# Local attention of the last stage: one matmul per head in quarter and eighth tiles, in place of head pairs padded with zeros

## The chip, the cores and the metric

The kernel runs on one core of a Trainium2 chip. The core has a matrix engine (TensorE; PE in the profile, its weight loads PEld), a vector engine (VectorE, DVE), an activation engine (ScalarE, ACT), a general engine (GpSimd, POOL) and a queue that issues DMAs (SyncE, SP). Each takes its own instructions strictly in the order in which they were written, and they wait for one another on semaphores. The metric is the time of one execution on the device in microseconds.

## The reference, cut to what matters

The network has eight parts on activations of 16 sequences of 256 tokens by 128 features. The change is in the last one, a small transformer with 6 layers, 16 heads of 64 and a window of 32 tokens, applied to each sequence:

```python
def local_attention(q, k, v):                 # (b, 16 heads, 256, 64)
    ...                                       # 8 windows of 32 queries; each sees 64 keys: the window before and its own
    sim = jnp.einsum('bhwie,bhwje->bhwij', bq, bk2) * QK_SCALE
    sim = jnp.where(mask, -jnp.finfo(sim.dtype).max, sim)
    attn = jax.nn.softmax(sim, -1)
    out = jnp.einsum('bhwij,bhwje->bhwie', attn, bv2)
...
    q = l2norm(q) * qs
    k = l2norm(k) * ksc
    q = q * cos * scale + rotate_half(q) * sin * scale      # rotate_half: (x1, x2) -> (-x2, x1)
    k = k * cos * inv + rotate_half(k) * sin * inv
    out = local_attention(q, k, v)
    return out.transpose(0, 2, 1, 3).reshape(b, n, INNER) @ Wo
```

Each layer adds this to the activations, then a feed-forward part (layer norm, 128 to 2 x 341, gelu gate, back to 128).

## The kernel before, in words

The last stage is the method `L3f`. A unit `u` is one sequence in one layer, 6 x 16 = 96 units in a row. A unit has two tiles `t` of 128 tokens. All is float32; the activations stand transposed in `Z`.

Each engine has a function (`pe`, `act`, `dve`, `pool`) that writes out its instructions for two units at a time. The lists at the end of these functions are an order written by hand: the work of unit 2i+1, 2i+2, 2i+3 and 2i+4 is interleaved in it, and nothing reorders it. One unit passes through these steps:

- `project` (L2559): 12 matmuls of 128x512 for q, k and v, into three PSUM banks in turn. ACT squares the q and k parts (L2768), DVE sums the squares per head (L2954), ACT takes the inverse root (L2776, L2778), DVE scales into `raw` (L2971, `norm`). ACT copies the v part (L2787), and SP puts it into windows (`vw`) by DMA.
- Rotation on POOL, four halves of a unit (q and k of each tile): `sine` (L3155) multiplies the swapped halves of each head by the sine table into `t2`, `cosine` (L3164) multiplies `raw` in place, `add` (L3172) adds. The swap is made by two instructions, each of 16 heads x 32.
- `turn_qk` (L2572): eight groups of four 128x128 transposes through one PSUM bank; after each group ACT copies the bank to SBUF (`turned`), q to `qz` (L2799) and k to `kT` (L2803), and the next group waits for the copy.
- `scores` (L2588): `qz` holds for each pair of heads and each window a block whose two diagonal quarters are the q of the two heads and whose other two are zero. So one matmul with 128 rows of contraction and 64 columns of weights does both heads of a window: 32 matmuls for each tile, in two column halves of the array.
- DVE adds the mask (L2982), takes the maximum (L2988) and subtracts it (L2996); ACT takes the exponential (L2810), DVE the sum (L3002), the reciprocal (L3008) and the product (L3014) in `sm`.
- `turn_p` (L2601): 8 transposes of 128x128 into PSUM banks 4 and 5; ACT spreads them to `pT` (L2820) with zeros in the same pattern, by four copies of 64 partitions each (`spread`).
- `values` (L2614): again 32 matmuls of 128 rows by 64 columns. ACT copies the outcome to `oT` (L2830), `project_out` (L2627) multiplies by Wo, then come the layer norm's matmuls (L2634, L2640) and, once in two units, the feed-forward part (L2653, L2660, L2669).

`halves` is ((partitions 0 to 63, 0), (partitions 64 to 127, 1)). A float32 matmul shows as two weight loads and two matmul records on TensorE, a transpose as one of each.

## Time and profile before

| what | us |
|---|---|
| the three runs | 4803.81, 4824.44, 4836.79 (median 4824.44) |
| span of the profiled execution | 4799.2 |
| the last stage within it | from about 1556 to the end |
| busy in the span: PE, DVE, ACT, POOL | 4554.0, 3761.7, 3501.1, 3692.6 |

A span is the time from the first to the last instruction of the profiled execution. A busy time of PE counts matmuls from the reading of their operands to their modelled end, so a PE that is busy all the time need not be streaming all the time.

### The profile page before, as it was taken

How to read it: one execution, taken by the hardware profiler on the slowest of the kernel's cores; microseconds unless marked ns; L12 is line 12 of the kernel's file. 1: busy time of each engine (PE TensorE's matmuls, PEld its weight loads, DVE VectorE, ACT ScalarE, POOL GpSimd, SP SyncE). 2: the span in 40 equal slices, each digit the busy share in tenths (PEclk: the TensorE clock that was granted, in tenths of full speed). 3: DMA queues.
4: the chain of work that ended last, by engine and by line, in shares of the span. 5: the costliest groups of instructions: out<-in, count | busy, mean ns of one | idle time of the engine just before them, and what ended most of it. 6: DMA issues, size and time to landing. Idle time of an engine off the chain costs nothing.

```text
span 4799.2 us, 114895 instructions
## 1 busy us (share of the span) xinstructions
PE 4554.0 (95%) x44512; PEld 3128.6 (65%) x44512; DVE 3761.7 (78%) x5226; ACT 3501.1 (73%) x6738; POOL 3692.6 (77%) x2336
## 2 busy tenths in 40 slices
PE   7998999987887799999999999999999999999997
PEld 5666768874443466666666666666666666666665
DVE  6776556658999688888888888888888888888885
ACT  3454756557775688888888888888888888888885
POOL 2222334438998999999999999999999999999993
PEclk9898999998999999999999999999999999999998
DMA  2000000004332222232222322232322322322222
GB/s 79 1 2 1 2 1 1 1 1 168 150 142 106 55 63 63 56 85 70 54 67 65 75 68 55 68 75 61 68 64 67 76 53 66 80 64 63 62 56 52
DMA packets 164292, 289.06 MB, mean 60 GB/s; under 512 B 44063, under 2 KB 61351, under 8 KB 159655
## 3 DMA queue, kind: packets, MB, share of 16 engines
q1 hardware_dynamic: 162310, 281.46, 22.3%
q8 instruction: 357, 5.85, 0.5%
q14 instruction: 185, 1.51, 0.1%
q10 hardware_dynamic: 1440, 0.24, 0.0%
HBM read 90.22 MB, written 2.62 MB: 19 GB/s over the span
## 4 chain that ended last, share of the span: by engine, by line
PE 59%; ACT 3%; issue 2%; DVE 1%; POOL 1%; ACTq 0%; DVEq 0%; POOLq 0%
PE ps L2559 18%; PE ps L2614 8%; PE ps L2588 8%; PE ps L2572 7%; PE ps L2627 7%; PE ps L2601 3%; PE ps L2669 3%; PE ps L2660 3%; PE ps L2653 3%; ACT L3f_pT L2820 2%; PE ps L2634 1%; PE ps L2640 1%; ACT L3f_kT L2803 1%; POOL L3f_t L3155 0%; POOL L3f_raw L3172 0%
## 5 line engine op out<-in xcount | busy, mean ns | idle before, releaser
L3155 POOL TENSOR_TENSOR L3f_t<-L3f_raw,L3f_rot 128x512 f32<-128x512 f32 x768 | 1007.7, 1334 | 268.3 <-DVE L3f_raw L2971 268.3
L2559 PE MATMUL ps<-L3f_wqkv,all_z 128*128 128x512 f32 x2304 | 1133.7, 601 | 12.8 <-DVE L3f_raw L2971 11.7
L3172 POOL TENSOR_TENSOR L3f_raw<-L3f_raw,L3f_t 128x1024 f32<-128x1024 f32 x384 | 961.4, 2504 | 3.8
L3164 POOL TENSOR_TENSOR L3f_raw<-L3f_raw,L3f_rot 128x1024 f32<-128x1024 f32 x384 | 953.8, 2484 | 3.8
L2971 DVE TENSOR_TENSOR L3f_raw<-ps,L3f_ri 128x512 f32<-128x512 f32 x768 | 495.6, 682 | 231.9 <-ACT L3f_ri L2778 230.2
L2954 DVE TENSOR_REDUCE L3f_ss<-L3f_sqr 128x8 f32<-128x512 f32 x768 | 507.8, 681 | 163.2 <-ACT L3f_sqr L2768 160.8
L2572 PEld LDWEIGHTS ps<-all_ident,L3f_raw 128*128 128x128 f32 x3072 | 358.7, 141 | 320.7 <-issue 282.8
L2559 PEld LDWEIGHTS ps<-L3f_wqkv,all_z 128*128 128x128 f32 x2304 | 385.2, 191 | 221.0 <-issue 151.5
L2572 PE MATMUL ps<-all_ident,L3f_raw 128*128 128x128 f32 x3072 | 472.3, 276 | 49.1 <-ACT L3f_kT L2803 27.1
L2820 ACT ACTIVATE L3f_pT<-ps 64x512 f32<-64x512 f32 x768 | 453.2, 590 | 83.9 <-PE ps L2601 75.9
L2768 ACT ACTIVATE L3f_sqr<-ps 128x512 f32<-128x512 f32 x768 | 449.9, 599 | 76.5 <-PE ps L2559 71.7
L2799 ACT ACTIVATE L3f_qz<-ps 64x512 f32<-64x512 f32 x768 | 451.5, 588 | 59.7 <-PE ps L2572 55.2
L2614 PEld LDWEIGHTS ps<-L3f_pT,L3f_vw 128*64 128x64 f32 x12288 | 377.4, 139 | 95.4 <-issue 50.9
L2614 PE MATMUL ps<-L3f_pT,L3f_vw 128*64 128x64 f32 x12288 | 404.0, 225 | 7.5 <-ACT L3f_pT L2820 7.5
L2588 PEld LDWEIGHTS ps<-L3f_kT,L3f_qz 128*64 128x64 f32 x12288 | 375.2, 138 | 52.5 <-issue 52.5
L2588 PE MATMUL ps<-L3f_kT,L3f_qz 128*64 128x64 f32 x12288 | 399.1, 223 | 0.0
L2803 ACT ACTIVATE L3f_kT<-ps 128x512 f32<-128x512 f32 x384 | 231.9, 604 | 164.7 <-PE ps L2572 163.5
L2627 PE MATMUL ps<-L3f_oT,L3f_wo 128*128 128x256 f32 x1536 | 349.3, 381 | 2.6 <-ACT L3f_oT L2830 2.6
L2627 PEld LDWEIGHTS ps<-L3f_oT,L3f_wo 128*128 128x128 f32 x1536 | 292.9, 191 | 84.5 <-issue 46.2
L3014 DVE TENSOR_TENSOR L3f_sm<-L3f_sm,L3f_sl 128x1024 f32<-128x1024 f32 x192 | 339.3, 1767 | 0.0
L2281 POOL TENSOR_TENSOR L3a_db_x<-L3a_dx,L3a_Bs 128x1024 f32<-128x1024 f32 x128 | 299.4, 2358 | 1.3 <-DMA L3a_Bs<-L3a_rows 1.1
L1916 PE MATMUL ps<-L3a_hc,all_ident 128*128 128x512 f32 x512 | 248.7, 633 | 39.0 <-DVE L3a_hc L2189 22.5
(333 smaller groups left out, 8702.0 us busy)
## 6 DMA issues: line engine op xcount, KB each, us to landing
L3f_vw<-L3f_v SPq DMA_DIRECT2D x1344, 128.0 KB, 2.4
L3a_Bs<-L3a_rows SPq DMA_DIRECT2D x16, 2048.0 KB, 7.1
L3a_Cs<-L3a_rows SPq DMA_DIRECT2D x16, 2048.0 KB, 11.6
L3f_vw<-L3f_v SPq DMA_DIRECT2D x192, 64.0 KB, 2.1
L3f_wqkv<-in_L_ffn_Wqkv SPq DMA_DIRECT2D x24, 256.0 KB, 2.9
L3f_wqkv<-in_L_ffn_Wqkv SPq DMA_DIRECT2D x6, 512.0 KB, 3.6
L3f_wo<-in_L_ffn_Wo SPq DMA_DIRECT2D x48, 64.0 KB, 2.3
out<-all_x SPq DMA_DIRECT2D x8, 256.0 KB, 3.6
```

What stands on the lines that cost most here:

```text
L2559: p.matmul(PS[:, j % 3, :], Z[:, u % NSEQ, t * P:t * P + P], w, start=True, stop=True).then_inc(proj.sem)
L2572: mm = p.transpose(PS[:, 3, c * P:c * P + P], raw[:, t, (4 * g + c) * P:(4 * g + c + 1) * P], ident[:, :])
L2588: mm = p.matmul(PS[r, 6 + w // 2, a * KEYS:(a + 1) * KEYS], qz[:, t, a, w, :, :].rearrange("p h q -> p (h q)"), kT[:, a, t * P + w * WIN:t ...
L2614: mm = p.matmul(PS[r * HD:(r + 1) * HD, 4 + c // 2, (c % 2) * 256 + w * HD:(c % 2) * 256 + (w + 1) * HD], vw[:, u % 2, t * NW + w, a * HD: ...
L2627: mm = p.matmul(PS[:, 4, 0:SEQ], wo[:, c, h, :], oT[:, :, c, :, h, :], start=(c + h == 0), stop=(c + h == PAIRS // 2))
L2799: op = a.activation(qz[r, t, 4 * g:4 * g + 4, :, half, :], src[r, :, :].rearrange("p c (w q) -> p c w q", q=WIN), ACT.Copy)
L2820: op = a.activation(pT[half * HD:(half + 1) * HD, t, r:2 * PAIRS:2, :, half, :], PS[r * HD:(r + 1) * HD, 4:6, :].rearrange("p b (n w h q) ...
L2954: v.tensor_reduce(ss[:, 0, i * UH:(i + 1) * UH], heads(sqr[:, i % 2, :]), AX.X, ALU.add).then_inc(ss_in.sem)
L2971: v.tensor_tensor(heads(raw[:, t, g * UNIT:(g + 1) * UNIT]), heads(PS[:, RING.index(x) % 3, :]), ri[:, i * UH:(i + 1) * UH].unsqueeze(2).b ...
L3155: op = g.tensor_tensor(t[:, :, to], r[:, :, fr], w[:, 1, to].unsqueeze(1).broadcast_to((P, H, WIN)), ALU.mult)
L3164: g.tensor_tensor(r, r, w[:, 0, :].unsqueeze(1).broadcast_to((P, H, HD)), ALU.mult).then_inc(cosined.sem)
L3172: g.tensor_tensor(r, r, t, ALU.add).then_inc(rotated.sem)
```

## The change

Queries are kept as they come from the transposes (`qT`), so scores are one matmul per head and window, with 64 rows of contraction and 32 columns of weights: 64 matmuls for a tile in place of 32. Likewise `pT` keeps the transposed probabilities as they are, and values are 64 matmuls with 64 rows, 64 columns and 32 moving columns. The first and second head of a pair now write different PSUM banks. ACT copies each group of q by one instruction of 128 partitions instead of two of 64, and each tile's probabilities by one of 128x1024 instead of four of 64x512. `sm` has another order of heads, so `below` writes through a permuted view; the mask table is half as large. `sine` is one instruction whose input runs over the two halves of each head with a negative step. The two memsets for the zeros are gone. Core of the diff:

```diff
             def scores(u, t):
...
                 for a in range(PAIRS):
                     for w in range(NW):
-                        r = slice(w % 2 * HD, w % 2 * HD + HD)
-                        mm = p.matmul(PS[r, 6 + w // 2, a * KEYS:(a + 1) * KEYS], qz[:, t, a, w, :, :].rearrange("p h q -> p (h q)"),
-                                      kT[:, a, t * P + w * WIN:t * P + w * WIN + KEYS], start=True, stop=True)
+                        for h, (r, _) in enumerate(halves):
+                            mm = p.matmul(PS[w * WIN:(w + 1) * WIN, 6 + h, a * KEYS:(a + 1) * KEYS], qT[r, t, a, w * WIN:(w + 1) * WIN],
+                                          kT[r, a, t * P + w * WIN:t * P + w * WIN + KEYS], start=True, stop=True)
...
             def values(u, t):
...
                 for c in range(PAIRS // 2):
                     for w in range(NW):
-                        for r in range(2):
-                            a = 2 * c + r
-                            mm = p.matmul(PS[r * HD:(r + 1) * HD, 4 + c // 2, (c % 2) * 256 + w * HD:(c % 2) * 256 + (w + 1) * HD],
-                                          vw[:, u % 2, t * NW + w, a * HD:(a + 1) * HD],
-                                          pT[:, t, w // 2 * PAIRS + a, w % 2, :, :].rearrange("p h q -> p (h q)"), start=True, stop=True)
+                        for to, n in halves:
+                            a = 2 * c + n
+                            for h, (r, _) in enumerate(halves):
+                                mm = p.matmul(PS[to, 4 + h, c * P + w * WIN:c * P + (w + 1) * WIN], vw[r, u % 2, t * NW + w, a * HD:(a + 1) * HD],
+                                              pT[r, t, a, w * WIN:(w + 1) * WIN], start=True, stop=True)
...
             def turned(u, t, g):
-                    for half in range(2):
-                        r = slice(half * HD, half * HD + HD)
-                        op = a.activation(qz[r, t, 4 * g:4 * g + 4, :, half, :], src[r, :, :].rearrange("p c (w q) -> p c w q", q=WIN), ACT.Copy)
+                    op = a.activation(qT[:, t, 4 * g:4 * g + 4, :], src, ACT.Copy)
...
             def spread(u, t):
-                for r in range(2):
-                    for half in range(2):
-                        op = a.activation(pT[half * HD:(half + 1) * HD, t, r:2 * PAIRS:2, :, half, :],
-                                          PS[r * HD:(r + 1) * HD, 4:6, :].rearrange("p b (n w h q) -> p (b n) w h q", w=2, h=2, q=WIN)[:, :, :, half, :], ACT.Copy)
-                op.then_inc(pT_in.sem)
+                a.activation(pT[:, t, :, :].rearrange("p a q -> p (a q)"), PS[:, 4:6, :].rearrange("p b n -> p (b n)"), ACT.Copy).then_inc(pT_in.sem)
...
             def below(u, t):
-                v.tensor_tensor(sm[:, t, :, :], sc(), mx[:, t, :].unsqueeze(2).broadcast_to((P, H, KEYS)), ALU.subtract).then_inc(s_sub.sem)
+                v.tensor_tensor(sm[:, t, :, :, :].rearrange("p a h k -> p h a k"), sc().rearrange("p (h a) k -> p h a k", h=2),
+                                mx[:, t, :].rearrange("p (h a) -> p h a", h=2).unsqueeze(3).broadcast_to((P, 2, PAIRS, KEYS)), ALU.subtract).then_inc(s_sub.sem)
...
             def sine(u, x):
-                for half in range(2):
-                    to, fr = slice(half * WIN, (half + 1) * WIN), slice((1 - half) * WIN, (2 - half) * WIN)
-                    op = g.tensor_tensor(t[:, :, to], r[:, :, fr], w[:, 1, to].unsqueeze(1).broadcast_to((P, H, WIN)), ALU.mult)
-                op.then_inc(sined.sem)
+                g.tensor_tensor(t.rearrange("p h (b e) -> p h b e", b=2), r.rearrange("p h (b e) -> p h b e", b=2)[:, :, ::-1, :],
+                                w[:, 1, :].rearrange("p (b e) -> p b e", b=2).unsqueeze(1).broadcast_to((P, H, 2, HD // 2)), ALU.mult).then_inc(sined.sem)
...
-        g.memset(qz[:, :, :, :, :, :], 0.0)
-        v.memset(pT[:, :, :, :, :, :], 0.0)
```

The hand-written order stays as it is. TensorE's rows at a place where the values of one unit are followed at once by the scores of the next are, before (shape as weight columns x moving columns, xN the matmuls of one kind in a row):

```order
L2614 MATMUL ps<-L3f_pT,L3f_vw 64x64 x32
L2588 MATMUL ps<-L3f_kT,L3f_qz 64x64 x32
L2601 MATMUL ps<-all_ident,L3f_sm 128x128 x8
L2559 MATMUL ps<-L3f_wqkv,all_z 128x512 x3
L2614 MATMUL ps<-L3f_pT,L3f_vw 64x64 x32
```

and after the change:

```order
L2615 MATMUL ps<-L3f_pT,L3f_vw 64x32 x64
L2588 MATMUL ps<-L3f_kT,L3f_qT 32x64 x64
L2601 MATMUL ps<-all_ident,L3f_sm 128x128 x8
L2559 MATMUL ps<-L3f_wqkv,all_z 128x512 x3
L2615 MATMUL ps<-L3f_pT,L3f_vw 64x32 x64
```

No row has moved; the number of matmuls in a group doubles, and two neighbouring groups that had one tile shape now have two. ScalarE's rows between two steps of the inverse root, before (`L3f_qz` and `L3f_pT` are the padded copies):

```order
L2799 ACTIVATE L3f_qz<-ps 64x16x32 x2
L2820 ACTIVATE L3f_pT<-ps 64x8x2x32 x4
L2803 ACTIVATE L3f_kT<-ps 128x4x128
L2768 ACTIVATE L3f_sqr<-ps 128x512
L2787 ACTIVATE L3f_v<-ps 128x512
L2768 ACTIVATE L3f_sqr<-ps 128x512
L2803 ACTIVATE L3f_kT<-ps 128x4x128
```

and after:

```order
L2797 ACTIVATE L3f_qT<-ps 128x512
L2817 ACTIVATE L3f_pT<-ps 128x1024
L2801 ACTIVATE L3f_kT<-ps 128x4x128
L2768 ACTIVATE L3f_sqr<-ps 128x512
L2787 ACTIVATE L3f_v<-ps 128x512
L2768 ACTIVATE L3f_sqr<-ps 128x512
L2801 ACTIVATE L3f_kT<-ps 128x4x128
```

Six ACT instructions become two at the same place, and all behind them stands closer.

## Rows read from the trace of the kernel before

**Rows 1.** Windows, 2000 to 4500 us: stretch length, then each engine's busy us

```profile
core 0: us, PE busy (x) PEld busy (x) DVE busy (x) ACT busy (x) POOL busy (x), PEclk, DMA share, GB/s
2000.00:4500.00 2500.00, 2473.85 (x27033) 1697.49 (x27030) 2067.85 (x2926) 2039.79 (x3825) 2276.34 (x1212) 1.00 0.28 67
```

**Rows 2.** The chain of work that ended last, 2000 to 4500 us, shares by line

```profile
by line: PE ps L2559 27.9%; PE ps L2614 11.9%; PE ps L2588 11.7%; PE ps L2572 11.3%; PE ps L2627 9.9%; PE ps L2601 4.0%; PE ps L2669 3.9%; PE ps L2660 3.9%; PE ps L2653 3.8%; issue 3.2%; ACT L3f_pT L2820 2.7%; PE ps L2634 1.3%; PE ps L2640 
```

**Rows 3.** Groups by line, same stretch: count, busy us, mean ns, idle before

```profile
line engine op names shapes xcount | busy us, mean ns | idle before us <-releasers
L3155 POOL TENSOR_TENSOR L3f_t<-L3f_raw,L3f_rot 128x512 f32<-128x512 f32 x606 | 795.3, 1334 | 217.7 <-DVE L3f_raw L2971 217.7
L3172 POOL TENSOR_TENSOR L3f_raw<-L3f_raw,L3f_t 128x1024 f32<-128x1024 f32 x303 | 758.9, 2505 | 3.0
L3164 POOL TENSOR_TENSOR L3f_raw<-L3f_raw,L3f_rot 128x1024 f32<-128x1024 f32 x303 | 754.1, 2489 | 3.0
...
L2820 ACT ACTIVATE L3f_pT<-ps 64x512 f32<-64x512 f32 x608 | 358.7, 590 | 63.5 <-PE ps L2601 57.2
L2799 ACT ACTIVATE L3f_qz<-ps 64x512 f32<-64x512 f32 x606 | 356.2, 588 | 46.3 <-PE ps L2572 42.8
...
L2803 ACT ACTIVATE L3f_kT<-ps 128x512 f32<-128x512 f32 x302 | 182.4, 604 | 126.9 <-PE ps L2572 125.9
...
L2830 ACT ACTIVATE L3f_oT<-ps 128x1024 f32<-128x1024 f32 x151 | 154.8, 1025 | 30.4 <-PE ps L2614 24.9
```

**Rows 4.** Timeline of TensorE, one group of values, then scores: start, length

```profile
3013.14 2.08 PE L2614 MATMUL ps<-L3f_pT,L3f_vw 128*64 128x64 f32 x64
...
3015.05 2.04 PE L2588 MATMUL ps<-L3f_kT,L3f_qz 128*64 128x64 f32 x64
```

**Rows 5.** Lines L2588, L2559, L899: ns of one record, min/median/max

```profile
L2588 PEld LDWEIGHTS ps<-L3f_kT,L3f_qz x12288: 132/138/231, 1589.6 to 4732.2; 128*64 128x64 f32 x199
L2588 PE MATMUL ps<-L3f_kT,L3f_qz x12288: 222/222/316, 1589.6 to 4732.2; 128*64 128x64 f32 x199
...
L2559 PEld LDWEIGHTS ps<-L3f_wqkv,all_z x2304: 186/190/338, 1556.0 to 4707.4; 128*128 128x128 f32 x192
L2559 PE MATMUL ps<-L3f_wqkv,all_z x2304: 590/592/1222, 1556.0 to 4707.8; 128*128 128x512 f32 x192
...
L899 PEld LDWEIGHTS ps<-L_sT,L_onz x512: 110/110/110, 480.5 to 634.6; 128*32 128x32 f32 x171
L899 PE MATMUL ps<-L_sT,L_onz x512: 272/273/273, 480.6 to 634.7; 128*32 128x128 f32 x171
```

**Rows 6.** Timeline of an earlier stage, four tiles of 32 columns side by side

```profile
480.36 0.13 PEld L896 LDWEIGHTS ps<-L_sT,L_vz 128*32 128x32 f32 x4
...
480.57 0.40 PE L899 MATMUL ps<-L_sT,L_onz 128*32 128x128 f32 x8
...
480.79 0.40 PE L896 MATMUL ps<-L_sT,L_vz 128*32 128x128 f32 x8
...
481.01 0.40 PE L899 MATMUL ps<-L_sT,L_onz 128*32 128x128 f32 x8
```

**Rows 7.** Timeline of an earlier stage, four tiles of 32 rows by 128 columns

```profile
483.59 1.17 PE L857 MATMUL ps<-L_qT,L_km 32*128 32x128 f32 x32
```

**Rows 8.** Timeline around a wait of TensorE for the spread of the probabilities

```profile
3009.41 2.40 ACT L2820 ACTIVATE L3f_pT<-ps 64x512 f32<-64x512 f32 x4
...
3011.84 0.60 ACT L2803 ACTIVATE L3f_kT<-ps 128x512 f32<-128x512 f32 x1
...
3012.58 0.63 PE L2572 MATMUL ps<-all_ident,L3f_raw 128*128 128x128 f32 x4 [0.54 <-ACT L3f_kT L2803]
```

**Rows 9.** Lines of POOL: ns of one instruction, min/median/max

```profile
L3155 POOL TENSOR_TENSOR L3f_t<-L3f_raw,L3f_rot x768: 1253/1277/2276, 1564.3 to 4710.9; 128x512 f32<-128x512 f32 x192
...
L3164 POOL TENSOR_TENSOR L3f_raw<-L3f_raw,L3f_rot x384: 2341/2366/3353, 1566.9 to 4714.4; 128x1024 f32<-128x1024 f32 x192
```

**Rows 10.** Timeline of the stage's start

```profile
1556.91 3.47 DVE L3203 MEMSET L3f_pT<- 128x4096 f32 x1 [1.21 <-PEq L91]
...
1558.01 0.60 ACT L2768 ACTIVATE L3f_sqr<-ps 128x512 f32<-128x512 f32 x1 [0.26 <-PE ps L2559]
1560.29 1.22 DVE L2954 TENSOR_REDUCE L3f_ss<-L3f_sqr 128x8 f32<-128x512 f32 x2
```

More of the change, by code:

```diff
@@ L2465, in L3f @@
         nc.vector.wait_ge(*got_m.at(0, 15))
-        nc.vector.tensor_copy(lmaskb[:, :, :, :], lmask).then_inc(made.sem)
+        nc.vector.tensor_copy(lmaskb[:, :, :], lmask).then_inc(made.sem)
         yield
@@ L2626, in project_out @@
                     for h in range(2):
-                        mm = p.matmul(PS[:, 4, 0:SEQ], wo[:, c, h, :], oT[:, :, c, :, h, :], start=(c + h == 0), stop=(c + h == PAIRS // 2))
+                        mm = p.matmul(PS[:, 4, 0:SEQ], wo[:, c, h, :], oT[:, :, h, c, :], start=(c + h == 0), stop=(c + h == PAIRS // 2))
                 mm.then_inc(w_mm.sem)
@@ L2809, in exponent @@
                 a.wait_ge(*s_sub.at(u, t))
-                a.activation(sm[:, t, :, :], sm[:, t, :, :], ACT.Exp, scale=QK_SCALE).then_inc(s_exp.sem)
+                x = sm[:, t, :, :, :].rearrange("p a h k -> p (a h k)")
+                a.activation(x, x, ACT.Exp, scale=QK_SCALE).then_inc(s_exp.sem)
             def spread(u, t):
@@ L2829, in output @@
                     a.wait_ge(*w_mm.at(u - 1))
-                a.activation(oT[:, t, :, :, :, :].rearrange("p c w h q -> p (c w h q)"), PS[:, 4:6, :].rearrange("p b n -> p (b n)"), ACT.Copy).then_inc(oT_in.sem)
+                a.activation(oT[:, t, :, :, :].rearrange("p h c q -> p (h c q)"), PS[:, 4:6, :].rearrange("p b n -> p (b n)"), ACT.Copy).then_inc(oT_in.sem)
             def centred(u):
@@ L2980, in hidden @@
                 v.wait_ge(*scored.at(u, t))
-                x = PS[:, 6:8, :].rearrange("p b (a k) -> p b a k", k=KEYS)
-                v.tensor_tensor(x, x, lmaskb[:, t, :, :].unsqueeze(2).broadcast_to((P, 2, PAIRS, KEYS)), ALU.add).then_inc(s_mask.sem)
+                v.tensor_tensor(sc(), sc(), lmaskb[:, t, :].unsqueeze(1).broadcast_to((P, H, KEYS)), ALU.add).then_inc(s_mask.sem)
             def top(u, t):
@@ L3001, in total @@
                 v.wait_ge(*s_exp.at(u, t))
-                v.tensor_reduce(sl[:, t, :], sm[:, t, :, :], AX.X, ALU.add).then_inc(s_sum.sem)
+                v.tensor_reduce(sl[:, t, :], sm[:, t, :, :, :].rearrange("p a h k -> p (a h) k"), AX.X, ALU.add).then_inc(s_sum.sem)
             def share(u, t):
@@ L3013, in scale @@
                 v.wait_ge(*s_inv.at(u, t))
[L3014 removed]
+                x = sm[:, t, :, :, :].rearrange("p a h k -> p (a h) k")
+                v.tensor_tensor(x, x, sl[:, t, :].unsqueeze(2).broadcast_to((P, H, KEYS)), ALU.mult).then_inc(s_mul.sem)
             def residual(u):
@@ L3197, in pool @@
             add(2 * i + 4, "k0")
-        g, v = nc.gpsimd, nc.vector
-        g.memset(vw[:, :, 0, :], 0.0).then_inc(zeroed.sem)
-        g.memset(kT[:, :, 0:WIN], 0.0)
-        g.memset(qz[:, :, :, :, :, :], 0.0)
-        v.memset(pT[:, :, :, :, :, :], 0.0)
+        nc.gpsimd.memset(vw[:, :, 0, :], 0.0).then_inc(zeroed.sem)
+        nc.gpsimd.memset(kT[:, :, 0:WIN], 0.0)
         for k in range(-1, N + 4):
@@ L3230, in constants @@
     first = seen & ((p[:, None] >= 32) | (k >= 32))
-    local = np.where(np.stack([first, seen], 1), 0.0, NEG).astype(np.float32)
-    local = local.reshape(2, 2, 1, 32, TILES, 64).repeat(2, axis=2)
-    c["c_local"] = np.ascontiguousarray(local.transpose(1, 2, 3, 4, 0, 5)).reshape(P, TILES, 2, 64)
+    c["c_local"] = np.where(np.stack([first, seen], 1), 0.0, NEG).astype(np.float32)
     hd, win = 64, 32
```

15 lines of the change are left out of this document (7 added, 8 removed).

## The prediction, made before the changed kernel ran

> **What bounds the kernel now.** I read the windows first. From 2000 to 4500 us, a stretch that lies wholly in the last stage, TensorE is busy for 2474 of 2500 us, POOL for 2276, DVE for 2068 and ACT for 2040, and the granted clock is full [rows 1]. A busy TensorE can be a waiting one, so the next view is the chain of work that ended last. There the reader should add up the PE lines: they and "issue" (TensorE waiting for nothing that the profile shows) make over 90% of the stretch, and the only other line that stands out is ScalarE's spread L2820 with 2.7% [rows 2]. So the stage is bound by TensorE. POOL's instruction count gives the scale: 303 `add`s at four to a unit are 76 units, 32.9 us each. All terms below are per unit, and there are 96.
>
> The next limit is POOL: 795.3 + 758.9 + 754.1 us over 76 units are 30.4 us, and its only real idle time is 217.7 us, 2.9 per unit, in which `sine` waits for DVE's `norm` [rows 3]. DVE has 27.2 and ACT 26.8 us of work per unit [rows 1].
>
> **What one round on TensorE costs.** A scores or values group of 64 records takes 2.08 us [rows 4]; less the 0.22 us of the last record alone [rows 5] that is 1.86 us, 58 ns for each pair of records on the two column halves. To see what sets 58 ns I take the records apart. A matmul record lasts 222 ns at 64 moving columns, 272 at 128 and 592 at 512: 0.83 ns per column, so 53 ns of streaming at 64 columns and 107 at 128, on top of a latency that is hidden. A weight load lasts 138 ns at 64 columns, 110 at 32 and 190 at 128, again some 0.8 to 0.9 ns per column: 53 ns and 28 ns [rows 5]. A pair now takes 58 ns because both the load and the stream of each half need 53. An earlier stage shows four column tiles: blocks of eight records follow each other every 0.22 us, so a round of four tiles takes 0.11 us, just the stream of one record of 128 columns, with the loads of 32 columns hidden [rows 6]. Row groups overlap as well: 32 records of 107 ns of streaming would be 3.4 us one after the other and took 1.17 us on four row tiles [rows 7]. My rule: a round over all tiles costs the longer of one load and one stream, plus 3 to 5 ns.
>
> **Scores.** 64 matmuls are 128 records, 16 rounds of eight tiles. A round has 53 ns of stream (64 moving columns) and 28 ns of load (32 columns): 56 to 58 ns, 0.92 us in all. Dispatch must keep up with eight records in 56 ns. Four weight loads of an earlier stage span 0.13 us where one alone takes 0.11 [rows 6], so they start 7 ns apart and eight need 53 ns; that just fits. Against 1.86 us a group saves 0.94, two groups in a unit save **1.9 us**. No row shows eight tiles at once or 128 such records in a row. From above the cost is bounded by the pace that rows 6 do show, 27 ns a record or 3.5 us a group; from below by dispatch at 7 ns, 0.9 us. I take 0.92, because the bursts inside a round show that 27 ns there is streaming and not dispatch.
>
> **Values.** Again 128 records, now 32 rounds of four tiles. The stream falls to 27 ns (32 columns) but the load is still of 64 columns, 53 ns. So a round costs 58 ns and the group 1.86 us: **nothing gained**. If the load did not bind, a round would be about 32 ns and a unit would gain 1.7 us; that is the low end.
>
> **One more switch of tile shape.** Where values are followed at once by scores, once in two units, there are now two shapes. "Issue" is 3.2% of 2500 us, 1.05 us a unit [rows 2], over about seven switches: 0.15 us each, so **+0.07**.
>
> **ScalarE.** Four copies of q per unit go from 2 x 0.588 to 0.604 us (L2803 is the same copy) and two spreads from 4 x 0.590 to 1.025 us (the size of L2830) [rows 3]: 2.3 + 2.7 = 5.0 us less, 26.8 to 21.8. ACT is not the bound, so only what TensorE waits for counts: the spread's 2.7% are 0.89 us a unit on the chain [rows 2]. At one such place four copies take 2.40 us, the k copy queued behind them starts after them, and the transposes wait 0.54 us for it [rows 8]. The chain's part should shrink to 1.03/2.36 of itself: **-0.5**. If the wait was for something else, this is 0.
>
> **POOL.** `sine` goes from 2 x 1334 ns to one instruction of 1024 elements, 2489 ns on average like `cosine` [rows 3]: 0.18 less, 0.7 in a unit, so POOL needs 29.7 us. No row has a negative step. The runs of 32 elements before cost the same per element as runs of 64 (1277 ns for 512, 2366 for 1024 [rows 9]), so I expect no price; the bounds are 2.37 us and, as a doubling, 5.1. This gains nothing by itself; it only lowers the next limit.
>
> DVE's `hidden`, `below`, `total` and `scale` touch the same 1024 elements in other orders: 0, and 5.7 us of DVE's slack would cover a mistake. DMAs are the same. The memset of `pT` holds DVE at the stage's start: its first sum comes at 1560.29 though its input was read from 1558.0 on [rows 10]; **-2 us** once.
>
> **Sum.** -1.9 + 0.07 - 0.5 is -2.35 us a unit: 32.9 to 30.55. But POOL at 29.7 would then be 97% busy, where it has 92% now, and its waits for `norm` would have to fall from 2.9 to 0.9 us. They should mostly fall, since `norm` comes late because TensorE and the squares on ACT are late, and both get ahead; but two engines at nearly the same load in a fixed order do not run without gaps. What is late next is `turn_qk`, which waits for POOL's `add`. I give back a quarter, 0.55 us. That leaves -1.8 us: 96 x 1.8 + 2 = 175 us. The profiled execution goes from 4799 to 4624. The median of the three runs is 25 us above that execution, and I subtract the same from it: 4824 - 175 = **4650 us**.
>
> **Rivals.**
> - *Eight tiles do not run side by side* (0.12). If TensorE keeps only four records in flight, scores have 32 rounds of 58 ns and gain nothing. Left are -0.5 + 0.07, times 96: 4780 us. For it: no row shows more than four at once. Against it: the number in flight was two with two tiles and four with four, so it follows the tiles.
> - *POOL takes over with its waits* (0.12). If `norm` stays as late relative to POOL as it is, the unit is 29.7 plus up to 2.9 us, 31.9 to 32.6: 4728 to 4795 us. For it: DVE and ACT waits stand between TensorE and POOL, and the order was written for the old durations. Against it: the waits end with ACT's inverse root, and ACT loses 5 us of work.
> - *TensorE cannot take records this fast for long; slower than before* (0.09). The place is scores and values. If 27 ns, the fastest sustained pace in rows 6, were a limit of the engine, each of the four groups would take 3.5 us instead of 1.86: +6.4 - 0.5 us a unit, about 5390 us. It decides from 14.5 ns a record on (1.86 us over 128), if all groups pay it. Against it stand the 7 ns steps; but only four follow in a row there.
> - *The negative step is slow* (0.03). POOL can take 2.5 us more a unit, 0.6 per `sine`. At a doubling it needs 30.4 + 4 x 2.5 = 40.4 us and bounds the stage: about 5540 us.
>
> The Trainium skill speaks for the third rival: the page "TensorE: Matmul & The Clock Gate", section "Wait — 56ns, not 53.3ns?", says that matmuls never start less than about 25 ns apart, however few columns they have. By that rule a group of 128 records is 3.2 us and the kernel ends near 5300 us, an estimate from the page's figure. The page "TensorEngine Tiling (Array Packing)", section "Instruction Overhead", likewise warns against cutting a dimension that is small already. By the 7 ns steps within a round [rows 6] the floor does not hold between different tiles; no row here shows it for long runs.
>
> **How the numbers follow.** The forecast has 0.64; its own range is 4590 (nothing given back) to 4720. The range for 8 in 10 is 4560 to 4790: the forecast with a little of the values' possible gain below, and the first two rivals above. About 1% is what a measurement of this kernel can tell from no change. Below 4776 lie the forecast and about half of the first two rivals: faster 0.77; within 1% 0.11; slower by over 1% 0.12.
>
> **What would show it.** In the changed kernel's profile: a scores group of 128 records in 1.1 to 1.2 us from first start to last end (forecast), 2.1 (first rival), 3.5 (third); a values group still at about 2.1; L2820's successor at 1.03 us and its share of the chain halved; `sine` at 2.4 to 2.6 us; a unit at 31.1 us with POOL over 95% busy. The prediction is wrong if values get shorter too, if a group shows pauses between rounds, or if POOL's waits stay near 2.9 us a unit.

## The result: slower by 1.6%, and the profile after

| | before | after | predicted |
|---|---|---|---|
| median, us | 4818.9 (4 runs, with the three of the table above) | 4895.4 (4 runs, 4875.9 to 4905.9) | 4650 (4560 to 4790) |
| after / before | 1 | 1.016, interval 1.012 to 1.020 | 0.964 |
| profiled execution, span in us | 4799.2 | 4904.6 | |

The time lies outside the range and on the other side. The windows of the changed kernel, for the stretch of [rows 1] (columns as there):

```profile
2000.00:4500.00 2500.00, 2371.13 (x45004) 1601.52 (x45004) 2000.22 (x2835) 1602.80 (x2979) 2159.61 (x882) 0.98 0.28 66
```

POOL now has 12 instructions per unit, so 882 are 73.5 units of 34.0 us; before, 1212 at 16 per unit give 33.0 (32.9 in the prediction, which rounds to 76 units), and the forecast was 31.1. All engines are busy for less, TensorE too. The granted clock is 0.98 here and was 1.00: by this, an estimate, TensorE was at its 1.2 GHz level for some 4% of the stretch. Part 3 of the page gives a cause to look for, the queue that brings instructions (packets, MB, share). Before:

```profile
q8 instruction: 357, 5.85, 0.5%
```

and after:

```profile
q8 instruction: 549, 8.99, 0.8%
```

A packet is 16 KB. The change adds 64 matmuls to each pair of a scores and a values group, 12,288 in all; a float32 matmul leaves two load and two matmul records, so that is 49,152 instructions more, and with 192 packets more there are 256 instructions in each. Groups by line of the changed kernel, 2000 to 4500 us (count, busy us, mean ns, idle before):

```profile
L3149 POOL TENSOR_TENSOR L3f_t<-L3f_raw,L3f_rot 128x1024 f32<-128x1024 f32 x294 | 728.1, 2476 | 334.6 <-DVE L3f_raw L2966 334.5
...
L2615 PE MATMUL ps<-L3f_pT,L3f_vw 64*64 64x32 f32 x18758 | 311.4, 221 | 18.8 <-issue 18.8
...
L2588 PE MATMUL ps<-L3f_kT,L3f_qT 64*32 64x64 f32 x18816 | 246.0, 229 | 94.5 <-issue 94.4
...
L2817 ACT ACTIVATE L3f_pT<-ps 128x1024 f32<-128x1024 f32 x147 | 149.6, 1017 | 126.3 <-PE ps L2601 126.3
```

The sine by a negative step (L3149) and the single spread (L2817) are as forecast. What is new is the idle time of TensorE ahead of its own scores and values, "issue": it waits for nothing that the profile shows, 113 us in these two lines. POOL's wait for `norm` (334.5 us, [rows 3] had 217.7) is the echo. Where the idle time lies is seen in the timeline of TensorE's matmuls, the place where values are followed by scores (start, length, count, idle before):

```profile
3003.28 1.48 PE L2615 MATMUL ps<-L3f_pT,L3f_vw 64*64 64x32 f32 x86
3006.37 1.49 PE L2615 MATMUL ps<-L3f_pT,L3f_vw 64*64 64x32 f32 x42 [1.61 <-issue]
3007.78 1.51 PE L2588 MATMUL ps<-L3f_kT,L3f_qT 64*32 64x64 f32 x85
3010.31 0.92 PE L2588 MATMUL ps<-L3f_kT,L3f_qT 64*32 64x64 f32 x43 [1.02 <-issue]
```

and of its loads at the same place:

```profile
3006.36 1.35 PEld L2615 LDWEIGHTS ps<-L3f_pT,L3f_vw 64*64 64x64 f32 x42 [1.72 <-issue]
3007.78 1.30 PEld L2588 LDWEIGHTS ps<-L3f_kT,L3f_qT 64*32 64x32 f32 x86
```

Two groups of 128 records are cut in pieces at places that have nothing to do with the work. From one pause to the next lie 42 + 86 loads and 42 + 85 matmul records: 255, one packet of instructions. It looks as if TensorE had run out of instructions twice. The whole stretch bears this out: count all loads and matmuls of TensorE from the start of the trace, and 86 of its 89 gaps of more than 0.9 us between two starts lie at one and the same place of a block of 256 (number 193). After each of these 86 the first record starts 1.1 to 1.6 us after a packet of that queue has ended, so the engine was waiting for that packet.

The granted clock belongs to this picture. From 2990 to 3003 us it is 1.00, and from 3003 to 3012 us, after a pause of 2.27 us at 2995.7 and with the two above, 0.69. So the 42 values records behind the first pause run partly at the 1.2 GHz level: they take 1.49 us, as long as the 86 before it.

### The profile page after: what moved, and what is told of

Same layout as the page of the kernel before. It is cut to its first block, busy times and chain, and to the rows that moved or that the text cites. A ratio compares the mean times of both kernels' runs of the same rounds, so it can differ in the third digit from the quotient of the medians.

```text
span 4904.6 us, 162701 instructions
## 1 busy us (share of the span) xinstructions
PE 4529.4 (92%) x69088; PEld 3075.2 (63%) x69088; DVE 3755.5 (77%) x5225; ACT 3010.1 (61%) x5778; POOL 3626.7 (74%) x1951
## 3 DMA queue, kind: packets, MB, share of 16 engines
q1 hardware_dynamic: 162310, 281.40, 21.8%
## 4 chain that ended last, share of the span: by engine, by line
PE 61%; issue 4%; DVE 1%; POOL 1%; ACT 1%; DVEq 0%; ACTq 0%; POOLq 0%
PE ps L2559 21%; PE ps L2615 8%; PE ps L2572 7%; PE ps L2627 7%; PE ps L2588 6%; PE ps L2601 4%; PE ps L2653 3%; PE ps L2660 3%; PE ps L2669 2%; PE ps L2634 1%; PE ps L2640 1%; DVE L3f_raw L2966 0%; POOL L3f_t L3149 0%; DVE L3f_ss L2949 0%; POOL L3f_raw L3166 0%
## 5 line engine op out<-in xcount | busy, mean ns | idle before, releaser
L3149 POOL TENSOR_TENSOR L3f_t<-L3f_raw,L3f_rot 128x1024 f32<-128x1024 f32 x384 | 950.7, 2476 | 429.9 <-DVE L3f_raw L2966 429.8
L2559 PE MATMUL ps<-L3f_wqkv,all_z 128*128 128x512 f32 x2304 | 1163.5, 615 | 19.2 <-DVE L3f_raw L2966 9.2
L2559 PEld LDWEIGHTS ps<-L3f_wqkv,all_z 128*128 128x128 f32 x2304 | 395.3, 195 | 248.4 <-issue 181.0
L2615 PEld LDWEIGHTS ps<-L3f_pT,L3f_vw 64*64 64x64 f32 x24576 | 384.9, 136 | 120.1 <-issue 115.9
L2588 PE MATMUL ps<-L3f_kT,L3f_qT 64*32 64x64 f32 x24576 | 321.6, 229 | 127.1 <-issue 126.9
L2615 PE MATMUL ps<-L3f_pT,L3f_vw 64*64 64x32 f32 x24576 | 409.1, 221 | 28.8 <-issue 25.3
L2588 PEld LDWEIGHTS ps<-L3f_kT,L3f_qT 64*32 64x32 f32 x24576 | 273.9, 107 | 198.8 <-issue 159.1
L2817 ACT ACTIVATE L3f_pT<-ps 128x1024 f32<-128x1024 f32 x192 | 195.4, 1018 | 173.2 <-PE ps L2601 173.2
L2825 ACT ACTIVATE L3f_oT<-ps 128x1024 f32<-128x1024 f32 x192 | 196.6, 1024 | 170.0 <-PE ps L2615 170.0
L2997 DVE TENSOR_REDUCE L3f_sl<-L3f_sm 128x16 f32<-128x1024 f32 x192 | 233.3, 1215 | 86.2 <-ACT L3f_sm L2809 85.4
```

Of the source, the lines that this page charges most:

```text
L2559: p.matmul(PS[:, j % 3, :], Z[:, u % NSEQ, t * P:t * P + P], w, start=True, stop=True).then_inc(proj.sem)
L2588: mm = p.matmul(PS[w * WIN:(w + 1) * WIN, 6 + h, a * KEYS:(a + 1) * KEYS], qT[r, t, a, w * WIN:(w + 1) * WIN], kT[r, a, t * P + w * WIN:t ...
L2615: mm = p.matmul(PS[to, 4 + h, c * P + w * WIN:c * P + (w + 1) * WIN], vw[r, u % 2, t * NW + w, a * HD:(a + 1) * HD], pT[r, t, a, w * WIN:( ...
L3149: g.tensor_tensor(t.rearrange("p h (b e) -> p h b e", b=2), r.rearrange("p h (b e) -> p h b e", b=2)[:, :, ::-1, :], w[:, 1, :].rearrange( ...
```

## The experiments

**Theories.** SUPPLY: instructions reach TensorE in blocks of 256, no faster than one per some 3.3 us (the closest spacing of the packets in the trace of the changed kernel), and only about one block is there ahead (what this "ahead" is worth is worked out under "Why the prediction was wrong"); a group that is now 256 instructions in 1.3 to 1.9 us of array work runs dry. TILES: small tiles are slow of themselves, wherever they stand and whatever brings them. POOL: its need, or its waits, hold the stage.

**TensorE alone.** Shortened; `scores(n)` issues n matmuls:

```
scores(1024)                          # 64x32 tiles, as in the stage
values(1024)                          # 64x64 tiles, 32 moving columns
full(1024)                            # 128x64 tiles
for wides in (4, 2, 1):
    for k in range(12):
        scores(64); wide(wides)       # wide: one matmul of 128x512
```

> None of the network is computed: after the inputs are loaded, TensorE alone runs sections with a wait between them, so its times say nothing of the network. Every float32 matmul is two weight loads and two matmuls, four instructions of TensorE's stream. (1) 1024 matmuls of 64x32 tiles as in the scores, (2) 1024 of 64x64 tiles with 32 columns as in the values, (3) 1024 of 128x64 tiles with 64 columns, (4) twelve bursts of 64 matmuls of 64x32 with 4 matmuls of 128x512 behind each, (5) the same with 2 behind each, (6) with 1. SUPPLY (instructions reach TensorE in blocks of 256, at most one per about 3.3 us, one block ahead): (1) and (2) 16 blocks each, 53 us, that is 26 ns per record, with a pause every 256 instructions; (3) bound by the array at 59.8 us (29 ns per record), the pauses almost gone; (4) no pauses, 6.7 us per burst; (5) 4.3 us per burst, hardly a pause; (6) 3.4 us per burst, with pauses. TILES (the small tiles themselves run no faster than their groups show in the changed kernel, whatever the supply): evenly spaced records, 9 to 17 ns each in (1), so 18 to 35 us, no pause at a fixed count, and 1.3 to 1.9 us for a burst in (6).

The page counts 22,052 instructions and 86 packets, 256 each. Timeline of the matmuls in the first section:

```profile
30.10 2.04 PE L127 MATMUL ps<-all_big 64*32 64x64 f32 x128 [1.69 <-issue]
33.83 2.04 PE L127 MATMUL ps<-all_big 64*32 64x64 f32 x128 [1.69 <-issue]
37.56 2.04 PE L127 MATMUL ps<-all_big 64*32 64x64 f32 x128 [1.69 <-issue]
41.29 2.04 PE L127 MATMUL ps<-all_big 64*32 64x64 f32 x128 [1.69 <-issue]
```

A pause of 1.69 us after every 128 records, 3.73 us per block, or 29 ns per record where I expected 26. The granted clock is 0.50 here, the 1.2 GHz level (it was 0.75 from 10 to 30 us and 0.50 from 30 us on, and TensorE had started with such pauses), so its array work is slower than in the kernel. The last bursts, with one wide matmul each, ran at the 2.4 GHz level:

```profile
328.86 1.12 PE L127 MATMUL ps<-all_big 64*32 64x64 f32 x91 [1.03 <-issue]
329.91 1.12 PE L147 MATMUL ps<-all_big 128*128 128x512 f32 x2
330.97 0.57 PE L127 MATMUL ps<-all_big 64*32 64x64 f32 x35
332.60 1.14 PE L127 MATMUL ps<-all_big 64*32 64x64 f32 x93 [1.07 <-issue]
```

A period of 260 instructions takes 3.74 us (328.86 to 332.60), of which TensorE works 2.7. So the pace is the same at both clock levels, some 3.7 us per 256 instructions; this belongs to the supply and not to the array. Other transfers don't explain it either: the DMA engines are busy for 2% here, against 28% in the stage. Bursts with four wide matmuls behind them have no pause:

```profile
199.00 1.48 PE L127 MATMUL ps<-all_big 64*32 64x64 f32 x128
200.41 3.70 PE L147 MATMUL ps<-all_big 128*128 128x512 f32 x8
204.04 1.48 PE L127 MATMUL ps<-all_big 64*32 64x64 f32 x128
```

They take 5.04 us each, less than my 6.7, since wide records follow each other in some 0.45 us and don't take the 0.6 that one lasts. With two wide matmuls a burst took 3.8 us for 264 instructions, again the supply. The section of 128x64 tiles shows why the kernel before did not meet this: 2048 records in 60.89 us and not one pause. They are 29.7 ns apart, and the supply brings one load and one matmul per 29 ns. The second section (58.1 us, 28 ns for each record) tells nothing, because at 1.2 GHz its array work takes about as long as its supply. A burst not cut by a pause lasts 1.48 us, 1.3 from first to last start, and not the 1.1 in all of the forecast: that is a second, smaller miss.

**Half of the matmuls, 722 instructions per unit as before the change.** Two windows' queries go against one window's keys:

```diff
-                    for w in range(NW):
+                    for w in range(0, NW, 2):
...
-                            mm = p.matmul(PS[w * WIN:(w + 1) * WIN, 6 + h, a * KEYS:(a + 1) * KEYS], qT[r, t, a, w * WIN:(w + 1) * WIN],
+                            mm = p.matmul(PS[w * WIN:(w + 2) * WIN, 6 + h, a * KEYS:(a + 1) * KEYS], qT[r, t, a, w * WIN:(w + 2) * WIN],
```

and the same in `values`.

> The changed kernel, but each scores and each values group is 32 matmuls instead of 64: two windows' queries (64) go against the keys of the first of the two windows, so the scores and values of every second window are not the reference's. All other work is the same, and TensorE has the instruction count of the kernel before. SUPPLY: with 722 instead of 1234 instructions per unit the pauses fall back to those of the kernel before, and the gain that was predicted appears: 4640 to 4700 us. TILES (small tiles are slow, or the single spread copy and the new layout bring nothing): no gain against before, 4780 to 4850. POOL (its sine waits for VectorE's norms, which are late for another reason): still about 4850 to 4900.

4644.5 us, 0.966 of before (0.962 to 0.969). As the supply wants it, but the scores and values groups are also shorter on the array than in the changed kernel (1.16 us each, not some 1.6 and 2.07), so this run alone doesn't tell the two apart. Hence the next three.

**Values alone in half.** The second of these two edits only:

```diff
             def values(u, t):
-                    for w in range(NW):
+                    for w in range(0, NW, 2):
```

> The changed kernel with the values in 32 matmuls of 64x64 with 64 columns per group: every second window's values are taken with the wrong keys and are not the reference's. It differs from the changed kernel in the 128 instructions per values group (978 per unit instead of 1234), while ScalarE's single spread copy stays. SUPPLY: 100 to 200 us below the changed kernel, 4690 to 4770 us, and between the two kernels with 722 and 1234 instructions. TILES or the layout at fault: 4850 or more.

4650.9 us, 0.969 (0.967 to 0.972). This run has 978 instructions per unit, and its scores still wait 64.8 us for "issue"; yet it is about as fast as the one with 722, and faster than the 4690 to 4770 us that I expected. POOL is busy for 94% in both, so I take it that TensorE, with the short values, has time to spare and a pause costs little; no run takes this apart.

**Scores alone in half.** The first edit only, in `scores`; here the values groups are just those of the changed kernel.

> The changed kernel with only the scores in 32 matmuls of 64x64 with 64 columns per group (every second window's scores are taken with the wrong keys); the values stay in 64 matmuls of 64x64 with 32 columns. 978 instructions per unit. SUPPLY: pauses only in the values groups, whose 256 instructions have 1.9 us of array work to hide behind; so between the kernel with 722 and the one with 1234, 4720 to 4800 us. TILES: 4850 or more if it is the narrow values that cost.

4694.2 us, 0.976 (0.972 to 0.979), again less than expected. TensorE's waits (us, times, longest):

```profile
PE ps L2588 <- issue: 22.1, 19, 1.6
...
PE ps L2615 <- issue: 9.2, 8, 1.5
```

31 us in place of 113, and a values group once more whole in 2.07 us. The unit is 2500 x 12 / 940 = 31.9 us.

**The predicted array time with the old instruction count.** To the half scores come values in 32 matmuls with 128 moving columns: 16 rounds of 107 ns in place of 32 rounds of 53.

```diff
-                                mm = p.matmul(PS[to, 4 + h, c * P + w * WIN:c * P + (w + 1) * WIN], vw[r, u % 2, t * NW + w, a * HD:(a + 1) * HD],
-                                              pT[r, t, a, w * WIN:(w + 1) * WIN], start=True, stop=True)
+                                mm = p.matmul(PS[to, 4 + h, c * P:(c + 1) * P], vw[r, u % 2, t * NW + w, a * HD:(a + 1) * HD],
+                                              pT[r, t, a, :], start=True, stop=True)
```

> The changed kernel with the array time that was predicted for it, in the instruction count of the kernel before (722 per unit): scores in 32 matmuls of 64x64 with 64 columns (about 1.1 us per group), values in 32 matmuls of 64x64 with 128 columns (16 rounds of about 110 ns, some 1.9 us per group). Every second window's scores and values are taken with the wrong keys and are not the reference's. If the prediction failed by the instruction supply alone, this is the kernel that it described: 4640 to 4700 us. If POOL or the chain through VectorE would have held it anyway: 4700 to 4780. If the array or the layout is at fault and not the number of instructions: 4850 to 4900.

4613.8 us, 0.959 (0.956 to 0.962). Its windows, and two of its groups in the timeline:

```profile
2000.00:4500.00 2500.00, 2469.55 (x28669) 1626.81 (x28668) 2149.29 (x3102) 1760.52 (x3256) 2393.75 (x964) 1.00 0.30 71
```

```profile
3010.41 1.98 PE L2615 MATMUL ps<-L3f_pT,L3f_vw 64*64 64x128 f32 x64
3012.28 1.16 PE L2588 MATMUL ps<-L3f_kT,L3f_qT 64*64 64x64 f32 x64
```

A values group of 1.98 us, a scores group of 1.16, a unit of 2500 x 12 / 964 = 31.1 us, POOL 96% busy: this is close to the kernel that the prediction described, and it takes about the time that was predicted (0.964 of before), even somewhat less; my expectation before this run, 4640 to 4700 us, was too high. It was 0.7 and 1.0% faster than the two kernels with still less array work. One difference is the granted clock, 1.00 here and 0.99 with half of all matmuls, where TensorE idles more; with half of the values it is 1.00 too, so that this isn't all. A fixed order that was fitted to other durations may explain the rest, but no run shows it.

**Same instructions, other order.** With the instructions of the changed kernel, seven of eight groups are issued in two halves:

```diff
-            scores(2 * i + 2, 0)
-            project(2 * i + 3, "v0b")
+            scores(2 * i + 2, 0, range(0, 4))
+            project(2 * i + 3, "v0b")
+            scores(2 * i + 2, 0, range(4, 8))
```

> The changed kernel, every instruction kept; only the order on TensorE differs: seven of the eight scores and values groups of two units are issued in two halves (64 records, 128 instructions each) with a projection (2 records, about 1.0 us) or four transposes between the halves. SUPPLY: 256 instructions now lie over 3 to 4 us of array work in most places, so the pauses at every 256th instruction shrink to a few tenths and the time falls well below the changed kernel, 4700 to 4790 us; if the new order holds ScalarE and VectorE up (they get scores and values about 1 us later), 4790 to 4850. TILES: the same records take the same time wherever they stand, so 4880 to 4910, or more by the two added changes of tile shape per group (0.07 us each, 8 per unit at most: +50 us).

4937.7 us, 1.029 (1.026 to 1.032): a miss. The waits of TensorE are

```profile
PE ps L2559 <- DVE L3f_raw L2977: 75.9, 75, 1.4
...
PE ps L2589 <- issue: 5.4, 10, 1.1
PE ps L2618 <- issue: 0.5, 2, 0.3
```

The pauses are all but gone with every instruction kept, so the supply was right in what it says of the pauses (TILES would have left them). Two things took the time. One is a new wait, 1.0 us per unit. A projection now stands in the middle of a group, and it must wait for VectorE's `norm`; the second half of the group waits behind it, and VectorE for that. The other is TensorE's own time: it is busy for 2394.4 us in 72.9 units, 32.8 us each, where the changed kernel has 32.3. One place of the timeline:

```profile
3017.18 1.12 PE L2559 MATMUL ps<-L3f_wqkv,all_z 128*128 128x512 f32 x2 [1.43 <-DVE L3f_raw L2977]
3018.24 0.86 PE L2589 MATMUL ps<-L3f_kT,L3f_qT 64*32 64x64 f32 x64
```

The same order over the old values did the same harm:

> The new scores with the old values (as in the run before), and the same split order. 978 instructions per unit. SUPPLY: the rest of the pauses goes, 4720 to 4770 us, no slower than without the split. TILES: 4770 to 4820 by the added shape changes and later groups.

4960.3 us, 1.033 (1.031 to 1.035), where the unsplit order takes 4766.6 (below). With only 978 instructions there was less to win, and the delay is whole. The clock is 1.00 in both, so this pair also shows what dividing costs TensorE itself: 32.8 us busy per unit against 31.7. That is 1.1 us for 3.5 divided groups per unit, with up to two more switches of tile shape each: some 0.16 us a switch, an estimate that puts all of it on the switches.

A second order takes first halves ahead of the work that stood before the group, where I expected the operands to be there early:

```diff
-            project(2 * i + 3, "v0a")
-            scores(2 * i + 2, 0)
+            scores(2 * i + 2, 0, range(0, 4))
+            project(2 * i + 3, "v0a")
+            scores(2 * i + 2, 0, range(4, 8))
```

> The changed kernel, every instruction kept, in another split order: of each divided group the first half goes ahead of the projection or of the four transposes that stood before it (their operands are there 1 to 2.6 us early), so that no second half stands behind a projection that waits for VectorE's norms, which is what held the first split order up. SUPPLY: pauses fall from 2 us to under 1 us per unit and nothing is late in their place: 4760 to 4850 us, below the changed kernel. TILES or order-blind: 4890 to 4940.

4837.6 us, 1.006 (1.004 to 1.008): some 50 us less than the changed kernel (1.006 against 1.016 of before) with the same instructions, which is what the order takes back, and still not less than before.

```profile
PE ps L2589 <- issue: 21.6, 29, 2.4
...
PE ps L2559 <- DVE L3f_raw L2978: 0.8, 2, 0.4
```

The new wait is gone, a fifth of the pauses is left and the clock is 1.00, but a unit is 33.3 us (x900 on POOL), not 32. TensorE is busy for 32.8 us of it, as in the first split order; with 4 divided groups per unit that is the cost of dividing once more. Whether it is the switches of tile shape, no run shows.

**The parts of the change.** The sine alone, in the kernel before:

> The kernel before with nothing but the one-operation sine by a negative step. If POOL's need of time had a share in the slowdown, it would show here. SUPPLY and TILES both: POOL waits for norms and isn't what ends last, so within 0.3% of before, 4800 to 4825, with the sine at 2.48 us as in the changed kernel. POOL: slower than before by 0.5% or more.

4797.8 us, 0.997 (0.995 to 0.998): a gain of 0.3%, small but measured, where I had said that it gains nothing by itself. The scores alone:

```diff
-                        for to, n in halves:
-                            a = 2 * c + n
-                            for h, (r, _) in enumerate(halves):
+                        for r in range(2):
+                            a = 2 * c + r
...
+                for half in range(2):
+                    r = slice(half * HD, (half + 1) * HD)
+                    op = a.activation(pT[r, t, :, :, half, :], PS[r, 4:6, :].rearrange("p b (n w q) -> p (b n) w q", w=NW, q=WIN), ACT.Copy)
```

> Only the scores in 64x32 tiles and the one query copy; the values as before, with a zeroed half, 32 matmuls of 128x64 per group, and two spread copies. 978 instructions of TensorE per unit (before 722, after 1234). SUPPLY: only half of the added instructions, so between the two: the scores groups of 256 instructions still meet pauses, the values no more; the scores still win about 1 us per unit of array time, so 4740 to 4830 us. TILES: scores groups as long as in the changed kernel, values groups 2.1 us, 4820 to 4870.

4766.6 us, 0.992 (0.990 to 0.993), faster than both kernels. Its TensorE rows are

```profile
3021.60 1.59 PE L2588 MATMUL ps<-L3f_kT,L3f_qT 64*32 64x64 f32 x128
...
3026.42 2.09 PE L2614 MATMUL ps<-L3f_pT,L3f_vw 128*64 128x64 f32 x64
```

So the edit of the values, for which I had written "nothing gained", costs some 120 us (1.016 against 0.992 of before, one spread copy less included): the same array time in twice the instructions. From this kernel to the changed one the unit grows by 1.6 us, of which 1.05 are pauses (127.8 in 73.5 units against 53.5 in 77.1) and 0.6 a longer busy time of TensorE. A whole values group is no longer than before, but the clock is 0.98 where it is 1.00 here, which allows for up to 0.7 us, an estimate (4% of the stretch at half speed). Two single moves on top of this kernel brought nothing clear of noise. The pauses in the scores fell from 45.8 to 33.6 us, by a quarter and not by the third to a half that I expected:

```diff
-            project(2 * i + 3, "v0a")
-            scores(2 * i + 2, 0)
+            scores(2 * i + 2, 0, range(0, 4))
+            project(2 * i + 3, "v0a")
+            scores(2 * i + 2, 0, range(4, 8))
...
             values(2 * i + 2, 0)
+            project(2 * i + 4, "k1a")
             scores(2 * i + 3, 1)
             turn_p(2 * i + 2, 1)
-            project(2 * i + 4, "k1a")
```

> The new scores with the old values, with two moves on TensorE: the scores of the even unit's first tile are split around the projection that stood ahead of them, and one projection goes between a values and a scores group that stood back to back. SUPPLY: the pauses of scores_only (0.6 us per unit) go down by a third to a half: 4720 to 4766 us, a little below scores_only. If the projection's delay of the scores counts more: 4766 to 4800.

4766.6 us, 0.990 (0.988 to 0.993).

**A kernel that is faster.** The changed kernel with five tiles in bfloat16, where a matmul is one load and one matmul record:

```diff
-        qT = self.sb("qT", [P, TILES, PAIRS, P])
+        qT = self.sb("qT", [P, TILES, PAIRS, P], BF16)
```

and the same for `kT`, `pT`, `vw` and `v2`.

> The changed kernel with the queries, keys, values and shares of the last stage kept in bfloat16 (five tiles; their precision is lower than in both other kernels, sums stay float32). The scores and values keep their 64 matmuls per group and the same tiles, but a bfloat16 matmul is one load and one matmul, 2 instructions instead of 4, so 722 per unit as in the kernel before. SUPPLY: no pauses, and the array time of the groups falls too, so POOL is the bound, as in the kernel with the predicted array time and 722 instructions: 4570 to 4640 us. TILES (64 small tiles per group are slow of themselves, whatever the number of instructions): 4750 to 4900.

4620.2 us, 0.959 (0.955 to 0.964). All 64 small matmuls of a group are there, in 722 instructions per unit:

```profile
2000.00:4500.00 2500.00, 2246.04 (x28736) 1387.69 (x28729) 2208.96 (x3103) 1747.28 (x3258) 2383.37 (x967) 0.98 0.16 39
```

```profile
3014.19 0.69 PE L2615 MATMUL ps<-L3f_pT,L3f_vw 64*64 64x32 bf16 x64
```

TensorE is busy for 9% less than in the kernel with the predicted array time, and the unit is 31.0 us all the same: with POOL at 95 to 96% in both, TensorE no longer sets the time. This run shows that 64 small matmuls in a group, at two instructions each, do no harm by their number; it doesn't weigh the supply by itself, since it also shortens the groups (0.69 us) and moves less by DMA (39 GB/s, not 66). And its clock is 0.98 almost without pauses: TensorE idles for 10% of the stretch, so a low clock goes with idle time here and not with pauses alone. The price is precision in the last stage's attention.

The runs in order of TensorE's instructions per unit (units from POOL's count in the windows; all against the kernel before on the same chip):

```
kernel                       instr.  unit us  ratio
before                          722     33.0  1
sine alone                      722     33.0  0.997
predicted array time            722     31.1  0.959
bfloat16                        722     31.0  0.959
half of all matmuls             722     31.5  0.966
half of the scores only         978     31.9  0.976
half of the values only         978     31.5  0.969
scores edit alone               978     32.4  0.992
the same, two moves             978     32.7  0.990
the same, first split order     978     34.8  1.033
second split order             1234     33.3  1.006
changed kernel                 1234     34.0  1.016
first split order              1234     34.3  1.029
```

## Why the prediction was wrong

**The bound.** Right: TensorE bound the stage, POOL comes next. The kernel with the predicted array time shows both, with POOL 96% busy and a unit of 31.1 us.

**The round on TensorE, scores.** Here it failed. "Dispatch must keep up with eight records in 56 ns ... that just fits" looked at the start of records within a round, 7 ns. That step is right: in the changed kernel half of the records of the scores start within 7 ns of the one before. What was not asked is how long such a pace can last. I priced a long run by the 27 ns of [rows 6] and put that down to streaming; for those rows it was, but the sustained supply is about the same, 29 ns per load and matmul. The kernel before lay just at it in its densest place (64 records of each of two groups, 128 loads and 128 matmuls, in 3.7 us), and nothing in its trace had to wait for it. The pauses measured 127.8 us over all lines of TensorE in 2500 us, 1.7 us per unit; the prediction had them at nothing.

How should the term read? It would not do to charge a dense place for its instructions less one block that lies ready. Values and scores back to back have 512 instructions; less a block 256 are left, 3.7 us, against 2.07 + 1.6 us of array work. That rule gives no pause there, and the trace has two. The packets say why. With TensorE alone a packet starts some 1.1 us (median) after TensorE has entered the block before the one that it brings, takes about 1.1 us, and its first record runs 1.4 us after its end. So nothing is saved up: each block of 256, wherever the count happens to cut, has to last for some 3.7 us, or TensorE waits for the difference. By this, 63 of the 86 pauses have their place, 101 of 146 us (from start to start, so a little more than the idle time). The other 23 follow blocks that had lasted 3.7 to 10.1 us already, because their packets began 3 to 10 us after TensorE had entered the block, and not 1; the pause at 3004.8 us above is one (its block began at 2997.9 and the packet at 3003.9). Ahead of 12 of these packets the kernel's own transfers kept the DMA engines busy, by 22 to 87% over 2 us, and ahead of the other 11 nothing moved at all. Why they were late stays open.

The Trainium skill, page "Runtime: NRT & Kernel Launch", section "Instruction fetch mechanics", says that instructions come in blocks of 256 and that fetching the next block is hidden, since the engine issues more slowly than blocks arrive. The first half is what the packets show (256 instructions each). The second does not hold here: the pauses stand one block or a multiple of it apart, and the measurement decides.

**The size of a scores group.** 0.92 us from first to last start was forecast; an undisturbed group takes 1.49 to 1.79 us in all, most often 1.6, so about 1.4. That is 0.9 us per unit, and with the pauses it makes 31.1 + 1.7 + 0.9 = 33.7, near the 34.0 measured. The sum leaves out the clock of 0.98, up to 0.7 us, and it adds waits as if none hid another, so its closeness is partly luck. What sets the length of the group isn't settled; one record in ten starts 17 ns or more after the one before.

**Values.** The array time was right, 2.07 us undisturbed where 2.08 was measured before, and the conclusion from it was wrong: "nothing gained" is a loss of some 120 us when the instructions double.

**The switch of shape (+0.07).** Not measured by itself. The price of 0.15 us a switch is near the 0.16 that the split order over the old values gives as an estimate.

**ScalarE.** The work is as forecast, 1602.8 / 73.5 = 21.8 us per unit and a spread of 1.02 us. That L2817 no longer ends TensorE's waits was also as forecast, but its worth of 0.5 us is only contained in the 31.1 of the kernel with the predicted array time and wasn't measured apart.

**POOL and the give-back.** The sine takes 2.48 us, as `cosine` does, so the negative step costs nothing. In the kernel with the predicted array time POOL waits 99.9 us for `norm`, 1.2 per unit; with the 0.9 that the prediction asked for it would have kept up wholly. The give-back of 0.55 was of the right size, if in that kernel only: -1.8 us per unit gives 31.1, and 31.1 was measured.

**The rivals.** The first falls: a scores group is shorter than with two tiles side by side. The second falls too: POOL's waits grew to 4.6 us per unit, but because TensorE was late, and they shrink when it isn't. The fourth falls by the row of L3149. The third had the right place and nearly the right pace, and the wrong price: it let all groups of the kernel pay 27 ns for each record, 6.4 us per unit, where many blocks of 256 take in wide matmuls beside a group and last as long as their supply. I gave it 0.09 since it looked like all or nothing. Taken in part, at the 1.7 and 0.9 us that were measured, it turns the forecast of -1.8 us per unit into +0.8. The rule of the Trainium skill that stood beside it (page "TensorE: Matmul & The Clock Gate", section "Wait — 56ns, not 53.3ns?"), no matmul sooner than about 25 ns after the last, is not what these traces show: within a group most start 5 to 12 ns apart. The pace over many blocks comes near that figure all the same, by another mechanism.

**What would show it.** "If a group shows pauses between rounds" named the sign that came, and so did the one on POOL: its waits went from 2.9 to 4.6 us per unit.

## What to carry to other kernels

Count instructions beside array time. Where a change cuts work into more and smaller matmuls, take the densest 256 instructions in a row, wherever they begin, and hold their array time against some 3.7 us; a float32 matmul counts four, a bfloat16 one two. Before trusting that small tiles pack well, look at part 3 of the page for the instruction queue and in the timeline for pauses marked "issue" that cut a group at odd counts, and look at the granted clock around them: a stretch with pauses can drop to the 1.2 GHz level (0.98 of full over the stage here), which lengthens the work beside them. And before moving work on TensorE to fill such pauses, check how early its operands are ready: a pause that was removed came back as a wait for another engine, and each divided group cost TensorE some 0.3 us of its own.

## What the runs showed of the hardware that was not expected

- TensorE got its instructions in packets of 16 KB, 256 each, with TensorE alone one per 3.7 us over a long run, at both clock levels alike. A packet started some 1.1 us after TensorE had entered the block before it, so no stock built up. Four wide matmuls (8 records, 3.6 us) behind a group of 256 instructions hid it, two did not.
- Tiles of 64x32 overlap well beyond two side by side: 128 loads and 128 matmuls took 1.48 us in a row, where 128x64 tiles need 3.8 for as many.
- TensorE's granted clock fell from 1.00 to 0.69 over 9 us with two pauses in them, and was 0.98 over the stretch, against 1.00 in the kernel before and in the second split order.
- POOL read with a negative step over blocks of 32 elements in 2476 ns for 1024 elements, against 2485 without one.
